# A two-layer network on one core: the carried states of a scan multiplied in 16-bit halves instead of float32

## The chip, the core and the metric

The kernel runs on one core of a Trainium2 chip. The metric is the time of the whole program on the device in microseconds (us), as the median of several runs. Five engines work side by side and meet at semaphores: TensorE (PE; its weight loads are shown apart, as PEld), VectorE (DVE), ScalarE (ACT), GpSimd (POOL) and SyncE (SP), which issues the DMAs.

## The reference

Four blocks follow each other, each one `x = layernorm(x + block(x))`: a Mamba2 mixer, a linear layer with dequantised weights, an attention with rotary positions, and a gated feed-forward. The change lies in the mixer. It has 2 sequences of 512 tokens, 128 heads of 64 channels in 8 groups, and chunks of 128 tokens:

```
dt  = clip(softplus(dt + dt_bias));  cs = cumsum(dt * A) in each chunk
xdt = x * dt
Ydiag  = (C B^T * exp(cs_l - cs_s), lower triangle) @ xdt
states = B^T @ (exp(cs_last - cs) * xdt)             # one per chunk and head
carry  = carry * exp(cs_last) + states               # from chunk to chunk
Yoff   = (C * exp(cs)) @ carry of the chunks before
Y = Ydiag + Yoff + x * D
```

After it come a gate `Y * silu(z)`, an RMS norm over a group and the output projection. The change is in how `Yoff` is multiplied: `C * exp(cs)` is the decayed C, `carry` the carried state.

## The kernel before

The mixer walks over 128 tiles. A tile is 128 channels (two heads) of one sequence, 512 tokens in 4 chunks. Eight tiles make a unit (one group, one sequence), two units a group of 16 tiles. Each engine has its own program of *slots*, one per tile (`slots`, line 672): slot 0, then a hardware loop of 7 rounds over `m = 1..16`, then 15 more. I call `m % 16` the slot's number. Each engine's order inside a slot is written out by hand, and semaphores alone tie the engines together.

TensorE in slot m: `scan(m)` (line 802) makes Y of tile m in PSUM. For each chunk it has one float32 product for each head with the matrix E (`Ydiag`, line 811, 128x64 weights and 128 columns), and, from the second chunk on, one for each head with the carried state `st` as weights and the decayed C `ecs` as columns (`Yoff`, line 815). The two heads take the left and right 64 columns of the array. Then `states(m+1)` (nine 16-bit products from `xw` and its rest `xwlo`), the x projection of tile m+3 (12 products of 512 columns), the z projection (`gate(m+1)`, 12), `turn_x(m+2)` (4 transposes), in slots 2 and 10 the B projection, in 4 and 12 the C projection (12 more each), and the output projection of tile m-1 (12). A float32 operand is taken as two 16-bit halves in these projections: `lead(w)` is the upper half of each word as bfloat16, `rest(w)` an fp16 remainder, and `product` (line 57) makes three 16-bit products of them.

VectorE in slot m (line 1171): waits for `y_ready` of `scan(m)`, `u = x*D + Y` (1176), `state(m+1, 0)` (1115), `u = u*gz` (1181), `state(m+1, 1..2)` (1120), E times the masked CB (`masked`, 1109), then `taps`: three convolution steps (256) with `remainder` (the rest of y, 1199) behind the first and `turned_x(m+2)` (x times dt, 1128) behind the second. In slots 0 and 8 it also adds the previous unit's output to the residual (1148), in 2, 4, 10 and 12 it has three more convolution steps, for B or C.

ScalarE in slot m (line 1023): in even slots two exponentials of E (996) behind a table load; the square of u (1002), `leading` (1005: y's leading half), in slots 0 to 7 the leading half of an output weight (230), the first convolution tap (243), eight `decays` (990), the gate's SiLU (1009, which gives `gz`, behind a table load in even slots), and the SiLU of x (248), which waits for the third convolution step.

GpSimd in slot m (line 1311): `decayed_C(m+1)` (1280, in place in `ecs`), in slots 0 to 7 the rest of an output weight (226), the sum of squares (1297), weight splits of the next group (`split`, 209: wx in slots 7 to 14, wz in 9 to 16), then `decayed_x(m+2)` (1285 `xw`, 1289 `xwlo`), which waits for `turned_x(m+2)` and which TensorE's `states(m+2)` needs in slot m+1. In the last unit (slots 120 to 127) `tail` adds the making of the linear layer's weights (lines 579 to 600).

`st` has two buffers, `ecs` four, E four, `xt` and `xw` two. `scan(m)` waits for E (`m_done`), the decayed C (`cs_done`) and `gz`.

Of the kernel before, what the change touches and what calls it, by code (L numbers as in the profile page):

```python
# [33 lines left out]
def lead(words):  # L34

    return words.bitcast(BF16)[..., 1::2]
# [594 lines left out]
def mixer(k, io, sc, aw):  # L631
# [3 lines left out]
    with ExitStack() as tmp:  # L635
        def sb(name, shape, dt=F32):
            return k.sb(name, shape, dt, tmp)
# [1 line left out]
        E = [sb(f"E{i}", [P, 2, CH, P]) for i in range(4)]  # L639
        xt = [sb(f"xt{i}", [P, CH, P]) for i in range(2)]  # L640
        xw = [sb(f"xw{i}", [P, CH - 1, P]) for i in range(2)]
        st = [sb(f"st{i}", [P, CH - 1, P]) for i in range(2)]
        u = [sb(f"u{i}", [P, T]) for i in range(2)]
        gz = [sb(f"gz{i}", [P, T]) for i in range(2)]
        yhi = [sb(f"yhi{i}", [P, T], F16) for i in range(2)]
# [3 lines left out]
        cbm = [sb(f"cbm{i}", [P, CH, P]) for i in range(NB)]  # L649
        bthi, btlo = ([sb(f"bt{n}{i}", [P, CH - 1, P], F16) for i in range(NB)] for n in ("hi", "lo"))  # L650
        xwlo = [sb(f"xwlo{i}", [P, CH - 1, P], F16) for i in range(2)]
        ms, rstd = sb("ms", [P, CH]), sb("rstd", [P, CH])
        lin = Linear(k, io, sc, (cbm[0][:].rearrange("p c t -> p (c t)"), acc[0][:]), tmp)
        norms = lin.norms
# [10 lines left out]
        ms_done, evac_done = S("ms_done"), S("evac_done")  # L665

        cs_done, xw_done, acc_done, rstd_done = S("cs_done"), S("xw_done"), S("acc_done"), S("rstd_done")
        acc_split, xw_lo, bt_done = S("acc_split"), S("xw_lo"), S("bt_done")

        Y, W, OUT = k.bank[2], k.bank[3], k.bank[4:8]  # L670
# [35 lines left out]
        with nc.Block() as block:  # L706
# [94 lines left out]
            def _(pe):  # L801
                def scan(t):

                    pe.wait_ge(m_done, t.n + 1)
                    pe.wait_ge(cs_done, t.n + 1)
                    pe.wait_ge(gz_done, t.n + 1)
                    for c in range(CH):
                        cols = slice(c * P, (c + 1) * P)
                        for h in range(2):
                            r = slice(h * HD, (h + 1) * HD)  # L810
                            mm = nc.tensor.matmul(Y[r, cols], xt[t.i % 2][:, c, r], E[t.i % 4][:, h, c], start=True, stop=c == 0,  # L811
                                                  skip_group_check=True)
                        for h in range(2 if c else 0):
                            r = slice(h * HD, (h + 1) * HD)
                            mm = nc.tensor.matmul(Y[r, cols], st[t.i % 2][:, c - 1, r], sc.ecs[t.i % 4][:, h, (c - 1) * P:c * P],  # L815
                                                  start=False, stop=True, skip_group_check=True)
                    mm.then_inc(y_ready, 1)

                def states(t):
# [164 lines left out]
            def _(act):  # L984
# [9 lines left out]
                def exps(t):  # L994
                    act.wait_ge(clip_done, t.n + 1)
                    nc.scalar.activation(E[t.i % 4][:], E[t.i % 4][:], ACT.Exp, scale=-1.0).then_inc(exp_done, 1)

                def square(t):
                    act.wait_ge(yg_done, t.n + 1)
                    if t.i:  # L1000
                        act.wait_ge(acc_done, t.n)
                    nc.scalar.activation((sq if t.i else acc[t.b])[:], u[t.i % 2][:], ACT.Square).then_inc(sq_done, 1)  # L1002
# [12 lines left out]
                def first():  # L1015
                    decays(tile_at(0, 0))
                    turned_B(tile_at(0, 0), OUT[3])
                    exps(tile_at(0, 0))
                    gate(tile_at(0, 0))
                    decays(tile_at(0, 1))  # L1020
                    decays(tile_at(0, 2))

                def slot(g, m):
                    s = tile_at(g, m)
                    if m % 2 == 0:
                        for d in (1, 2):
                            if tile_at(g, m + d):
                                exps(tile_at(g, m + d))
                    square(s)
                    leading(s)  # L1030
                    if m % 16 < XT:

                        sc.lead_wo(act, s.g, m % 16)
                    t, nu = tile_at(g, m + 3), next_unit(s)
                    if t:
                        q = conv_of_slot(s, "x")

                        wait(act, y_done, s.n)
                        sc.tap(act, q, ring_bank(s.b, x_use(s)), sc.xc[t.i % 4], t.g, t.b, 2 + t.i)
                        if not (isinstance(g, int) and g == 0 and m == 0):  # L1040
                            decays(t)
                    if tile_at(g, m + 1):
                        gate(tile_at(g, m + 1))
                    if t:
                        sc.silu(act, q, sc.xc[t.i % 4])
                    if isinstance(g, int) and g == 0 and m == 0:
                        decays(t)
                    if nu and s.i == 2:
                        act.wait_ge(bt_ready, s.u + 1)
                        sc.tap(act, conv_of_slot(s, "B"), ring_bank(s.b, USE_B), sc.xcB, nu.g, nu.b, 0)  # L1050
                        sc.silu(act, conv_of_slot(s, "B"), sc.xcB)
                    if nu and s.i == 4:
                        sc.tap(act, conv_of_slot(s, "C"), ring_bank(s.b, USE_C), sc.xcC[nu.b], nu.g, nu.b, 1)
                        sc.silu(act, conv_of_slot(s, "C"), sc.xcC[nu.b])
                    if nu and s.i == 6:
                        turned_B(nu, k.bank[ring_bank(s.b, USE_BT)])
                    if is_last_unit(s):
                        tail(s)
# [45 lines left out]
            def _(dve):  # L1104
# [7 lines left out]
                def state(t, c):  # L1112
                    if c == 0:
                        dve.wait_ge(st_ready, t.n + 1)
                        nc.vector.tensor_copy(st[t.i % 2][:, 0], W[:, 0:P]).then_inc(s_step, 1)
                        return
                    dve.wait_ge(s_step, 3 * t.n + c)
                    for h in range(2):
                        r = slice(h * HD, (h + 1) * HD)
                        mm = nc.vector.scalar_tensor_tensor(  # L1120
                            out=st[t.i % 2][:, c, r], in0=st[t.i % 2][:, c - 1, r], scalar=head(sc.cd, t, c, h),
                            in1=W[:, c * P + h * HD:c * P + (h + 1) * HD], op0=ALU.mult, op1=ALU.add)
                    mm.then_inc(s_step, 1)

                def turned_x(t):

# [33 lines left out]
                def first():  # L1160
                    dve.sem_inc(ms_done, 1)
                    dve.sem_inc(evac_done, 4)
                    turned_x(tile_at(0, 0))
                    masked_CB(tile_at(0, 0), ring_bank(1, USE_CB))
                    rest_of_B(tile_at(0, 0), OUT[3])
                    for c in range(CH - 1):
                        state(tile_at(0, 0), c)
                    masked(tile_at(0, 0))
                    turned_x(tile_at(0, 1))

                def slot(g, m):
# [10 lines left out]
                    if n1:  # L1182
                        state(n1, 1)
                        state(n1, 2)
                        masked(n1)
                    if ended:
                        mean_square(s.u, s.b)

# [11 lines left out]
                                                       in1=yhi[s.i % 2][:], op0=ALU.mult, op1=ALU.subtract).then_inc(lo_done, 1)  # L1200

                    if n3:
                        taps("x", sc.xc[n3.i % 4], n3, 2 + n3.i, (remainder, lambda: turned_x(n2)))
                    else:
                        remainder()
                        if n2:
                            turned_x(n2)
# [67 lines left out]
            def _(pool):  # L1275
                def decayed_C(t):
                    pool.wait_ge(sc.ecs_in[t.i % 2], (t.g * 8 + (t.b * 4 + t.i // 2 + 1)) * 16)
                    pool.wait_ge(sc.xc_done, conv_of_C(t) + 1)
                    e = sc.ecs[t.i % 4]
                    nc.gpsimd.tensor_tensor(e[:], e[:], sc.xcC[t.b][:, P:T].unsqueeze(1).to_broadcast([P, 2, T - P]),  # L1280
                                            ALU.mult).then_inc(cs_done, 1)

                def decayed_x(t):
                    pool.wait_ge(xt_done, t.n + 1)
# [26 lines left out]
                def slot(g, m):  # L1311
# [9 lines left out]
                    if more:  # L1321
                        if mm == 4:
                            sc.split_bc(pool, s.g + 1, 0)
                        if mm == 6:
                            sc.split_bc(pool, s.g + 1, 1)
                        if 7 <= mm <= 14:
                            sc.split_wx(pool, s.g + 1, mm - 7)
                        if 9 <= mm:
                            sc.split_wz(pool, s.g + 1, mm - 9)
                    if m == 16:  # L1330
                        sc.split_wz(pool, s.g, XT - 1)
                    if tile_at(g, m + 2):
                        decayed_x(tile_at(g, m + 2))
                    if is_last_unit(s):
                        tail(s)

# [1031 lines left out]
```

## Time and profile before

| | us |
|---|---|
| median of 3 runs (lowest, highest) | 2432.82 (2430.52, 2433.77) |
| the profiled execution | 2433.26 |
| its span, first to last instruction | 2431.4 |
| busy in the span: PE, DVE, ACT, POOL | 2343.2 (96%), 1794.1 (74%), 1584.3 (65%), 1377.3 (57%) |

The trace's timeline gives the start of each scan. These are the starts in one round of the loop, for slot numbers 0 to 15 and the next 0, in us from the span's start: 970.69, 981.66, 992.46, 1005.72, 1016.22, 1029.32, 1040.71, 1051.54, 1062.04, 1072.74, 1083.25, 1096.34, 1106.84, 1119.94, 1131.33, 1142.16, 1152.67. So a plain slot lasts 10.50 us, one with a B or C projection 13.09 to 13.26, slots 5 and 13 last 11.39, 6 and 14 10.83, 8 10.70, and 0 and 1 10.97 and 10.80. The mixer runs from about 57 us to 1515 us, the linear layer to 1560, attention and feed-forward to the end.

How to read it: busy times of one engine overlap a little (an instruction starts before the one before it has ended), and a PE that is busy is only one whose pipeline holds something. What a slot costs is the distance between two scan starts.

### The profile page before, as it was taken

The numbers are of one execution on the slowest core, as the hardware profiler recorded it, in microseconds if no ns is written. First come the engines' busy times: TensorE is split into PE (matmuls) and PEld (weight loads), VectorE is DVE, ScalarE is ACT, GpSimd is POOL, SyncE is SP. The second block draws the span as 40 slices with busy tenths as digits, with TensorE's granted clock in tenths as the row PEclk, the third lists the DMA queues.
The fourth block names the chain that finished last, engine by engine and source line by source line (L and its number), as shares of the span: only waits on it lengthen the run. The fifth ranks groups of instructions, "written<-read, shape, count | busy, mean of one in ns | idle before, by whom it ended". The sixth has DMA issues, their size and how long they took to land. (4 is left out here: it accounts for less than half of the span.)

```text
span 2431.4 us, 49850 instructions
## 1 busy us (share of the span) xinstructions
PE 2343.2 (96%) x16008; PEld 1328.4 (55%) x16008; DVE 1794.1 (74%) x3250; ACT 1584.3 (65%) x3327; POOL 1377.3 (57%) x1178
## 2 busy tenths in 40 slices
PE   6999999999999999999999998879999999999898
PEld 3555555555555555555555554445555556555444
DVE  6777777777777787777777885567787777888613
ACT  6776776776776776776776774355665555655533
POOL 5576576576576576576576579344344434454323
PEclk8999999999999999999999999889999999999999
DMA  7343343343343343343343441320010110100000
GB/s 244 120 134 113 111 136 113 112 137 111 111 137 111 110 136 113 112 137 111 112 137 110 132 152 36 129 89 14 36 40 14 41 36 14 40 10 14 1 1 35
DMA packets 117294, 218.95 MB, mean 90 GB/s; under 512 B 10016, under 2 KB 43424, under 8 KB 115840
## 3 DMA queue, kind: packets, MB, share of 16 engines
q1 hardware_dynamic: 116992, 215.29, 27.0%
q8 instruction: 145, 2.38, 0.4%
q14 instruction: 157, 1.29, 0.2%
HBM read 212.10 MB, written 3.15 MB: 89 GB/s over the span
## 5 line engine op out<-in xcount | busy, mean ns | idle before, releaser
L990 ACT ACTIVATE E<-wq,cst 128x128 f32<-128x128 f32 x1024 | 311.7, 389 | 2.2 <-PEq L298 2.2
L256 DVE SCALAR_TENSOR_TENSOR xc<-bank,taps,xc 128x511 f32<-128x511 f32 (+2 forms) x384 | 283.0, 737 | 24.6 <-ACT xc L243 24.1
L1963 POOL TENSOR_TENSOR qT<-qT,qrot 128x512 f32<-128x512 f32 x64 | 81.3, 1270 | 358.3 <-DVE qrot L1852 358.3
L1297 POOL TENSOR_TENSOR acc<-acc,sq 128x512 f32<-128x512 f32 x112 | 162.6, 1452 | 183.5 <-ACT sq L1002 183.5
L61 PE MATMUL bank<-xhi,wx 128*128 128x512 f16 x640 | 242.7, 379 | 0.0
L60 PE MATMUL bank<-xlo,wx 128*128 128x512 f16 x640 | 242.6, 379 | 0.0
L59 PE MATMUL bank<-xhi,wx 128*128 128x512 f16 x640 | 242.5, 379 | 0.0
L1109 DVE TENSOR_TENSOR E<-E,cbm 128x1024 f32<-128x1024 f32 x128 | 235.0, 1836 | 0.9
L1280 POOL TENSOR_TENSOR ecs<-ecs,xcC 128x768 f32<-128x768 f32 x128 | 235.2, 1837 | 0.4 <-POOLq L298 0.4
L1176 DVE SCALAR_TENSOR_TENSOR u<-xc,D,bank 128x512 f32<-128x512 f32 x128 | 95.7, 747 | 177.1 <-PE bank L815 166.4
L1285 POOL TENSOR_TENSOR xw<-xt,wdec 128x384 f32<-128x384 f32 x128 | 106.5, 832 | 174.5 <-DVE xt L1128 174.4
L811 PE MATMUL bank<-E,xt 128*64 128x128 f32 x2048 | 185.6, 280 | 14.6 <-issue 7.3
L1002 ACT ACTIVATE sq<-u 128x512 f32<-128x512 f32 x112 | 70.5, 629 | 196.8 <-DVE u L1181 195.5
L59 PE MATMUL bank<-xhi,wz 128*128 128x512 f16 x512 | 195.3, 381 | 0.4 <-DVE u L1176 0.3
L60 PE MATMUL bank<-xlo,wz 128*128 128x512 f16 x512 | 195.2, 381 | 0.0
L61 PE MATMUL bank<-xhi,wz 128*128 128x512 f16 x512 | 195.1, 381 | 0.0
L59 PE MATMUL bank<-wohi,yhi 128*128 128x512 bf16 x512 | 194.2, 379 | 0.0
L60 PE MATMUL bank<-wolo,yhi 128*128 128x512 f16 x512 | 194.2, 379 | 0.0
L61 PE MATMUL bank<-wohi,ylo 128*128 128x512 bf16 x512 | 194.2, 379 | 0.0
L1780 ACT ACTIVATE probs<-bank,nmx 128x512 f32<-128x512 f32 (+3 forms) x256 | 131.5, 526 | 67.6 <-DVE nmx L1882 67.6
L811 PEld LDWEIGHTS bank<-E,xt 128*64 128x64 f32 x2048 | 120.2, 137 | 64.6 <-issue 62.1
L209 POOL TENSOR_TENSOR wx<-wx 128x512 f16<-128x512 f32 x80 | 147.7, 1850 | 10.5 <-DMA wx<-in_w_xbc 10.5
(265 smaller groups left out, 6617.3 us busy)
## 6 DMA issues: line engine op xcount, KB each, us to landing
wq<-cs_rows SPq DMA_DIRECT2D x128, 512.0 KB, 4.0
ecs<-ecs_rows SPq DMA_DIRECT2D x128, 384.0 KB, 3.6
wx<-in_w_xbc SPq DMA_DIRECT2D x80, 256.0 KB, 2.6
wz<-in_w_z SPq DMA_DIRECT2D x64, 256.0 KB, 2.6
wo<-in_w_o SPq DMA_DIRECT2D x64, 256.0 KB, 3.9
wq<-in_wq SPq DMA_DIRECT2D x8, 1024.0 KB, 5.6
awo_raw<-in_wo SPq DMA_DIRECT2D x32, 256.0 KB, 3.0
wkv<-in_wkv SPq DMA_DIRECT2D x8, 512.0 KB, 3.7
```

Of the source, the lines that this page charges most:

```text
L59: nc.tensor.matmul(out, lhs[0], rhs[0], start=first, stop=False, skip_group_check=skip)
L60: nc.tensor.matmul(out, lhs[0], rhs[1], start=False, stop=False, skip_group_check=skip)
L61: return nc.tensor.matmul(out, lhs[1], rhs[0], start=False, stop=last, skip_group_check=skip)
L209: self.nc.gpsimd.tensor_tensor(rest(w), w, lead(w), ALU.subtract).then_inc(sem, 1)
L256: self.nc.vector.scalar_tensor_tensor(out=dst[:, d:T], in0=self.k.bank[bank][:, 0:T - d], scalar=self.taps[:, bass.ds(g, 1), b, j, 3 - d:4 ...
L811: mm = nc.tensor.matmul(Y[r, cols], xt[t.i % 2][:, c, r], E[t.i % 4][:, h, c], start=True, stop=c == 0, skip_group_check=True)
L990: ins = nc.scalar.activation(E[t.i % 4][:, h, c], sc.csr[t.i % 2][:, h, c * P:(c + 1) * P], ACT.Relu, scale=-1.0, bias=head(sc.cst, t, c, h))
L1109: nc.vector.tensor_tensor(e, e, cbm[t.b][:].rearrange("p c t -> p (c t)").unsqueeze(1).to_broadcast([P, 2, T]), ALU.mult).then_inc(m_done, 1)
L1280: nc.gpsimd.tensor_tensor(e[:], e[:], sc.xcC[t.b][:, P:T].unsqueeze(1).to_broadcast([P, 2, T - P]), ALU.mult).then_inc(cs_done, 1)
L1285: nc.gpsimd.tensor_tensor(by_head(xw[t.i % 2][:]), by_head(xt[t.i % 2][:, 0:CH - 1]), of_heads(sc.wdec, t, 0, CH - 1), ALU.mult).then_inc( ...
L1297: nc.gpsimd.tensor_tensor(acc[t.b][:], acc[t.b][:], sq[:], ALU.add).then_inc(acc_done, 1)
L1780: ins = nc.scalar.activation(pr[h % 2][:, P_OFF[i]:P_OFF[i] + (i + 1) * P], k.bank[bank][:, at:at + (i + 1) * P], ACT.Exp, bias=nmx[h % 2] ...
```

## The change

The carried states and the decayed C are each split into two 16-bit halves, and the two float32 products for a chunk become six 16-bit ones, in the order head 0, head 1 for each of three terms. The halves of the state are made on ScalarE (`sthi`, fp16) and VectorE (`stlo`, fp16), the rest of the decayed C on GpSimd (`ecslo`, fp16; its leading half is read in place). `st`, `sthi`, `stlo` and `ecslo` have one buffer each. On VectorE `turned_x` moves from behind the second convolution step to behind the first, and `remainder` from the first to the second. On GpSimd `decayed_x` moves ahead of the split of wz.

```diff
-        st = [sb(f"st{i}", [P, CH - 1, P]) for i in range(2)]
+        st = sb("st", [P, CH - 1, P])
+        sthi, stlo = sb("sthi", [P, CH - 1, P], F16), sb("stlo", [P, CH - 1, P], F16)
...
+        ecslo = sb("ecslo", [P, 2, T - P], F16)
...
                 def scan(t):
                     pe.wait_ge(m_done, t.n + 1)
-                    pe.wait_ge(cs_done, t.n + 1)
+                    pe.wait_ge(cs_lo, t.n + 1)
+                    pe.wait_ge(st_lo, t.n + 1)
                     pe.wait_ge(gz_done, t.n + 1)
...
-                        for h in range(2 if c else 0):
-                            r = slice(h * HD, (h + 1) * HD)
-                            mm = nc.tensor.matmul(Y[r, cols], st[t.i % 2][:, c - 1, r], sc.ecs[t.i % 4][:, h, (c - 1) * P:c * P],
-                                                  start=False, stop=True, skip_group_check=True)
+                        e, d = sc.ecs[t.i % 4], slice((c - 1) * P, c * P)
+                        for x in range(3 if c else 0):
+                            for h in range(2):
+                                r = slice(h * HD, (h + 1) * HD)
+                                mm = nc.tensor.matmul(Y[r, cols], (sthi, sthi, stlo)[x][:, c - 1, r],
+                                                      (lead(e[:, h, d]), ecslo[:, h, d], lead(e[:, h, d]))[x],
+                                                      start=False, stop=x == 2, skip_group_check=True)
...
+                def leading_states(t):
+                    act.wait_ge(s_step, 3 * t.n + 3)
+                    nc.scalar.copy(sthi[:], st[:]).then_inc(st_hi, 1)
...
                     square(s)
                     leading(s)
+                    if tile_at(g, m + 1):
+                        leading_states(tile_at(g, m + 1))
...
+                def rest_of_states(t):
+                    dve.wait_ge(st_hi, t.n + 1)
+                    nc.vector.tensor_tensor(stlo[:], st[:], sthi[:], ALU.subtract).then_inc(st_lo, 1)
...
                         masked(n1)
+                        rest_of_states(n1)
...
-                        taps("x", sc.xc[n3.i % 4], n3, 2 + n3.i, (remainder, lambda: turned_x(n2)))
+                        taps("x", sc.xc[n3.i % 4], n3, 2 + n3.i, (lambda: turned_x(n2), remainder))
...
                     nc.gpsimd.tensor_tensor(e[:], e[:], sc.xcC[t.b][:, P:T].unsqueeze(1).to_broadcast([P, 2, T - P]),
                                             ALU.mult).then_inc(cs_done, 1)
+                    pool.wait_ge(cs_done, t.n + 1)
+                    wait(pool, y_ready, t.n)
+                    nc.gpsimd.tensor_tensor(ecslo[:], e[:], lead(e[:]), ALU.subtract).then_inc(cs_lo, 1)
...
-                        if 9 <= mm:
-                            sc.split_wz(pool, s.g + 1, mm - 9)
+                    if tile_at(g, m + 2):
+                        decayed_x(tile_at(g, m + 2))
+                    if more and 9 <= mm:
+                        sc.split_wz(pool, s.g + 1, mm - 9)
                     if m == 16:
                         sc.split_wz(pool, s.g, XT - 1)
-                    if tile_at(g, m + 2):
-                        decayed_x(tile_at(g, m + 2))
```

## Rows read from the trace of the kernel before

**Rows 1.** Stretches, us: length, busy PE, PEld, DVE, ACT, POOL; clock, DMA share, GB/s

```profile
970.69:1152.67 181.98, 181.46 (x1320) 102.77 (x1319) 140.51 (x234) 133.52 (x259) 119.55 (x93) 1.00 0.39 120
1436.32:1493.85 57.53, 50.59 (x379) 28.98 (x378) 43.15 (x73) 35.14 (x68) 54.95 (x50) 1.00 0.33 112
```

**Rows 2.** Timeline of PE in slot 3: start, duration, line, operation, [idle before it]

```profile
1005.72 0.66 PE L811 MATMUL bank<-E,xt 128*64 128x128 f32 x8
1006.21 0.39 PE L815 MATMUL bank<-ecs,st 128*64 128x128 f32 x4
1006.42 0.39 PE L811 MATMUL bank<-E,xt 128*64 128x128 f32 x4
...
1007.47 0.22 PE L60 MATMUL bank<-xwlo,bthi 128*128 128x128 f16 x1
1007.52 0.22 PE L61 MATMUL bank<-xw,btlo 128*128 128x128 bf16 x1
```

**Rows 3.** Weight loads and a matmul by line: ns least, median, most; first and last start

```profile
L815 PEld LDWEIGHTS bank<-ecs,st x1536: 136/137/231, 57.7 to 1510.5; 128*64 128x64 f32 x192
L815 PE MATMUL bank<-ecs,st x1536: 272/273/421, 57.8 to 1510.6; 128*64 128x128 f32 x192
L861 PEld LDWEIGHTS bank<-xcC,xcB x128: 189/192/337, 47.6 to 1404.0; 128*128 128x128 f32 x128
```

**Rows 4.** Timeline of ACT in slot 8 (scan starts at 1062.04)

```profile
1061.71 0.63 ACT L248 ACTIVATE xc<-xc 128x512 f32<-128x512 f32 x1 [1.21 <-DVE xc L256]
1063.65 2.01 ACT L996 ACTIVATE E<-E 128x1024 f32<-128x1024 f32 x2
1065.56 0.61 ACT L1002 ACTIVATE acc<-u 128x512 f32<-128x512 f32 x1
1066.09 0.70 ACT L1005 ACTIVATE yhi<-u,nw 128x512 f16<-128x512 f32 x1
1067.39 0.78 ACT L243 ACTIVATE xc<-bank,taps 128x512 f32<-128x512 f32 x1 [0.60 <-PE bank L61]
1068.07 2.43 ACT L990 ACTIVATE E<-wq,cst 128x128 f32<-128x128 f32 x8
1071.82 0.60 ACT L1009 ACTIVATE gz<-bank 128x512 f32<-128x512 f32 x1
```

**Rows 5.** Timeline of DVE in slots 8 and 9 (scans start at 1062.04, 1072.74)

```profile
1063.93 0.75 DVE L1176 SCALAR_TENSOR_TENSOR u<-xc,D,bank 128x512 f32<-128x512 f32 x1 [2.25 <-PE bank L815]
1064.79 0.68 DVE L1181 TENSOR_TENSOR u<-u,gz 128x512 f32<-128x512 f32 x1
...
1074.66 0.75 DVE L1176 SCALAR_TENSOR_TENSOR u<-xc,D,bank 128x512 f32<-128x512 f32 x1 [0.30 <-PE bank L815]
```

**Rows 6.** Timeline of POOL and DVE where two of their instructions meet, slot 2

```profile
994.21 1.83 POOL L1280 TENSOR_TENSOR ecs<-ecs,xcC 128x768 f32<-128x768 f32 x1
...
995.24 1.35 DVE L1181 TENSOR_TENSOR u<-u,gz 128x512 f32<-128x512 f32 x1
```

**Rows 7.** The nearest instructions to the added ones, by line

```profile
L1289 POOL TENSOR_TENSOR xwlo<-xw x128: 825/826/829, 49.7 to 1495.8; 128x384 f16<-128x384 f32 x128
L226 POOL TENSOR_TENSOR wolo<-wo x64: 1038/1040/1958, 61.4 to 1417.1; 128x512 f16<-128x512 f32 x64
L1138 DVE TENSOR_TENSOR btlo<-bank,bthi x16: 557/558/560, 50.9 to 1415.3; 128x384 f16<-128x384 f32 x16
L1013 ACT CAST bthi<-bank x16: 469/471/478, 50.4 to 1414.8; 128x384 f16<-128x384 f32 x16
```

**Rows 8.** Timeline of PE: the scan of slot 2, behind slot 1

```profile
992.46 0.66 PE L811 MATMUL bank<-E,xt 128*64 128x128 f32 x8 [0.23 <-ACT gz L1009]
```

**Rows 9.** Timeline of POOL and PE before the last scans

```profile
1491.94 1.80 POOL L1280 TENSOR_TENSOR ecs<-ecs,xcC 128x768 f32<-128x768 f32 x1
...
1507.23 1.80 POOL L1280 TENSOR_TENSOR ecs<-ecs,xcC 128x768 f32<-128x768 f32 x1
...
1493.85 1.12 PE L811 MATMUL bank<-E,xt 128*64 128x128 f32 x8 [5.67 <-issue]
```

More of the change, by code:

```diff
@@ L667, in mixer @@
         cs_done, xw_done, acc_done, rstd_done = S("cs_done"), S("xw_done"), S("acc_done"), S("rstd_done")
+        st_hi, st_lo, cs_lo = S("st_hi"), S("st_lo"), S("cs_lo")
         acc_split, xw_lo, bt_done = S("acc_split"), S("xw_lo"), S("bt_done")
@@ L1019, in first @@
                     gate(tile_at(0, 0))
+                    leading_states(tile_at(0, 0))
                     decays(tile_at(0, 1))
@@ L1114, in state @@
                         dve.wait_ge(st_ready, t.n + 1)
-                        nc.vector.tensor_copy(st[t.i % 2][:, 0], W[:, 0:P]).then_inc(s_step, 1)
+                        nc.vector.tensor_copy(st[:, 0], W[:, 0:P]).then_inc(s_step, 1)
                         return
@@ L1120, in state @@
                         mm = nc.vector.scalar_tensor_tensor(
-                            out=st[t.i % 2][:, c, r], in0=st[t.i % 2][:, c - 1, r], scalar=head(sc.cd, t, c, h),
+                            out=st[:, c, r], in0=st[:, c - 1, r], scalar=head(sc.cd, t, c, h),
                             in1=W[:, c * P + h * HD:c * P + (h + 1) * HD], op0=ALU.mult, op1=ALU.add)
                     mm.then_inc(s_step, 1)
+                def rest_of_states(t):
+                    dve.wait_ge(st_hi, t.n + 1)
+                    nc.vector.tensor_tensor(stlo[:], st[:], sthi[:], ALU.subtract).then_inc(st_lo, 1)
                 def turned_x(t):
@@ L1168, in first @@
                     masked(tile_at(0, 0))
+                    rest_of_states(tile_at(0, 0))
                     turned_x(tile_at(0, 1))
```

## The prediction

> **What bounds the kernel now.** I read the stretches first [rows 1]: in one round of the mixer's loop (16 slots, 181.98 us) PE is busy 181.46 us, DVE 140.5, ACT 133.5, POOL 119.6. So PE sets the time, and an instruction added elsewhere costs nothing while something covers it. In the last unit it is different: in slots 121 to 125 (57.53 us) POOL is busy 54.95 and PE 50.59. Then I read single slots in the timelines, because the shares of a round hide a chain that is nearly as long as a slot: scan, DVE's u, ACT's square and y, first tap, eight decays, gz, next scan. In slot 8 gz ends at 1071.82 + 0.60 = 1072.42 and the scan starts at 1072.74, 0.32 later; the chain's other slack is the 0.60 that ACT waits for PE's projection before the first tap [rows 4]. Behind slot 1 the scan already waits for gz [rows 8]. DVE has 2.25 us of rest before u in slot 8, but only 0.30 in slot 9, behind the residual adds [rows 5].
>
> **The change, part by part.**
>
> *PE.* The 4 records of one chunk's float32 products (two heads, two records each) take from 1006.21 to 1006.42, 0.21 to 0.22 us [rows 2]. Four of them span 0.39 us: 0.11 from the first pair to the second, 0.273 for one record [rows 3], nearly nothing left for a distance inside a pair. So the two heads' halves of the array run side by side. In 16 bits a product of 128 columns takes 1007.52 - 1007.47, 0.05 to 0.06 us [rows 2]. If the pairs stay side by side, three terms take 3 x 0.057 = 0.17 against 0.218: 0.047 saved on each of 3 chunks, 0.14 us a slot. Bounds: below, 6 x 0.057 = 0.34 a chunk if the two heads run one behind the other, 0.37 us lost a slot; above, 3 x 0.05, 0.2 us gained. I take 0.14, the row of 16-bit products with the pairing of the float32 ones.
>
> What speaks against it are the weight loads. A float32 load of 128 columns is 192 ns, one of 64 columns 137 [rows 3]: 55 ns for 64 columns, just under one product's 57. The Trainium skill (TensorEngine Tiling, Restrictions and Gotchas) says that tiling the columns switches the fast weight load off. By that rule the new loads take the 55 ns too, hidden only if both heads load at once; no row here shows a 64-column load in 16 bits. Loaded one behind the other they would give 6 x 55 = 0.33 us a chunk, which is rival C.
>
> *ACT.* `leading_states` is a copy of 128x384 into fp16. The nearest row is 471 ns, out of PSUM [rows 7]; its neighbours overlap by about 0.05 to 0.1, so 0.42 net (0.38 to 0.5). It stands ahead of the first tap, in the chain above.
>
> *DVE.* `rest_of_states` is 128x384, near the 558 ns of btlo [rows 7], 0.50 net (0.4 to 0.6), and more where POOL holds it up. It stands behind `masked` and ahead of all taps.
>
> *POOL.* ecslo is 768 elements. From 384 to 512 elements this form grows from 826 to 1040 ns [rows 7], 1.67 ns an element, so 768 take 0.826 + 384 x 0.00167 = 1.47 us (1.3 to 1.83, the latter being the multiply of 768 elements [rows 6]). By its new wait it starts when scan(m) is done or, in the slots where `decayed_C` comes late, when that has ended. Behind the wait are queued the output weight's split, the sum of squares, the wx split and `decayed_x`. They have POOL's rest to fall into: 181.98 - 119.55 = 62 us a round, against 16 x 1.53 = 24.
>
> *The two meet.* In slot 2 `u*gz` takes 1.35 instead of 0.68 us while POOL's tensor_tensor runs from 994.21 to 996.04; it ends at 996.59, 0.55 behind POOL [rows 5, 6]. So VectorE's operation with two operands in SBUF waits until POOL's has ended and then needs its 0.55. ecslo starts at the end of the scan, and `u*gz` 0.86 us after u starts. Put into slot 8: scan ends at about 1063.8, ecslo holds until 1065.3 or, behind a late `decayed_C`, 1066.2; `u*gz` ends at 1065.85 to 1066.75 instead of 1065.47. That is 0.4 to 1.3 us, 0.8 in the middle, in almost every slot. I find nothing that excludes it.
>
> *The two moves.* `turned_x` a place earlier gives xw 0.7 to 0.8 us sooner, and the wz split no longer stands in front of it. That pays back what DVE's lateness takes from `states`. `remainder` is needed a slot later and costs nothing. But the third convolution step still ends behind all of it, and with it the SiLU of x, after which ACT begins the next slot. The added waits of the scan for `cs_lo` and `st_lo` cost nothing outside the last unit: ecslo ends some 3 to 5 us, stlo some 8 to 9 us into a slot of 10.4.
>
> **The sum.** Slot 8, worked out: in slot 7 DVE's third step ends later by 0.8 (behind ecslo) and 0.5 (stlo), its 2.25 us of rest hides that for u, but not for the SiLU; less 0.14 for the shorter scan this is 1.2. ACT's SiLU, table load and exponentials, which end at 1065.66 [rows 4], end at 1066.9; square, y and the new copy bring the first tap to 1066.9 + 0.53 + 0.62 + 0.42 = 1068.5 + 0.1, against 1067.39: 1.2 late. Of that 0.32 is covered before the scan, so slot 8 grows by 0.9. The others by the same steps: slot 6, where the longer slot 5 covers the SiLU but the copy of the output weight fills the 0.60, 0.7; slot 14, without that copy, 0.3; slot 0, as 8 but with it, 1.2; slot 1, where nothing is covered and DVE comes late from the residual, 1.4; slot 10, where DVE, late since slot 9's 0.30 of rest [rows 5], gives xw late for `states`, 0.8; slot 12, 0.3. Together 5.6. In the other 9 slots PE keeps its 0.14: -1.3. So 4.3 us a round, and for the 120 slots before the last unit 7.5 x 4.3 = 32.
>
> In the last unit scan 126 starts at 1493.85, 0.11 after `decayed_C` [rows 9], behind 5.67 us of idle PE. Here ecslo is straight in the path: 6 of them from slot 121 on, 6 x 1.53 = 9.2, less some 1.7 of the 2.58 us that POOL has free there [rows 1]: 7.5 us. (Bounds 6 and 10.)
>
> The profiled execution took 2433.26 us, 1.9 more than its span and 0.4 more than the median, which I leave aside. 2433.3 + 32 + 7.5 = 2473 us.
>
> **The rivals.**
>
> *B: the cover holds.* ecslo and `u*gz` don't keep each other waiting as in rows 6, or the chain has more slack than I found. Then PE's gain is all that is left: 120 x 0.14 = 17 us less, 7.5 more at the end: 2424 us. If the last unit hides its share too, 2415. For it: PE's share of a round and the free time of all the others [rows 1]. Against it: slot 8's 0.32 and the wait behind slot 1 [rows 4, 8].
>
> *C: the 16-bit pairs are slower than float32.* Loads or columns of the two heads behind each other: 0.33 a chunk is 0.11 more than before, 0.34 a slot, and 0.48 more than I took. In the 9 slots in which PE sets the time this is 4.3 us a round, 32 in all, of which about a third is given back where the other chains wait for the same PE: 2495 us. Against it: the float32 pairs run side by side [rows 2, 3].
>
> *D: a wash.* ecslo comes early enough in half of the slots and the copies overlap more than I think: 4.3 falls to about -1 a round, 2433.3 - 8 + 7.5 = 2433 us.
>
> The point from which the sign turns: the slots lose 5.6 us a round against PE's 16 x 0.14 = 2.3. With a loss of 1.3 a round the last unit's 7.5 just balances the gain.
>
> **How the numbers follow.** The forecast has 0.62, its own range 2452 to 2502: below, copies at 0.38 and 0.4 and ecslo at 1.3, which take some 2.5 us off a round; above, ecslo at 1.83, which puts POOL itself behind in slots 9 to 14, where wx and wz are both split, some +3.5 a round. B has 0.17, C 0.10, D 0.08, and 0.03 is left to something slower still. A change of 0.2%, 4.9 us, is about what can be told from none. Faster 0.18 (B), same 0.07 (most of D), slower 0.75. The range reaches down to B, as only so 8 in 10 is held, and up to the forecast's bound: 2422 to 2502.
>
> **What would show it.** The records of the three terms, 18 a tile, 64 columns wide: right if pairs start 0.05 to 0.06 us apart, C if 0.11. `u*gz` near 1.1 to 1.9 us instead of 0.68, and ending 0.55 after ecslo: the contention is right. Scan starts in a round: slot 8 at 11.6 instead of 10.70, 3, 7, 9, 15 at 10.36, the round near 186.3 instead of 181.98. Behind slots 0, 1, 6 and 8 the scan's wait ends with gz. In the last unit the scans 126 and 127 start 0.1 us after an ecslo, and the stretch from scan 120 on is some 7.5 us longer. The prediction is wrong if `u*gz` keeps to 0.68, or if the rounds are shorter than 181.98.

## The result and the profile after

The changed kernel takes 2476.25 us (median of four runs) against 2432.27 for the kernel before on the same chip; the recorded ratio is 1.0174, 95% interval 1.0159 to 1.0188. One of the four runs took 8239.14 us, was disturbed and is left out of the ratio (the other three are 2475.83, 2475.89 and 2476.61), as is one of 12170.60 us of the kernel with the copy alone below. The profiled execution has a span of 2474.0 us, 42.6 longer than before. The engines' totals, from the page of the changed kernel (busy us, share of the span, instructions):

```profile
PE 2320.4 (94%) x16579; PEld 1324.8 (54%) x16776; DVE 1974.7 (80%) x3378; ACT 1627.7 (66%) x3455; POOL 1613.8 (65%) x1306
```

I cut the span at three scans. From scan 0 to scan 120 it grew from 1368.3 to 1405.0 us (+36.7), from scan 120 to scan 127 from 83.5 to 94.0 (+10.5), and the rest shrank from 922.3 to 917.6 (-4.6). That rest lies behind the mixer; over all kernels built here it varies between 916.5 and 922.3 without a pattern that I can name, so I leave it aside. The windows answering to [rows 1] are slots 80 to 95 and, here, scan 120 to scan 127 (columns as there):

```profile
996.41:1183.93 187.52, 178.95 (x1400) 101.82 (x1415) 164.11 (x251) 138.69 (x274) 148.97 (x109) 1.00 0.37 116
1462.38:1556.35 93.97, 74.01 (x567) 43.32 (x574) 70.54 (x108) 56.06 (x102) 86.09 (x75) 0.93 0.26 87
```

The reader is to see that PE works less (178.95 against 181.46 us) in a longer round: it idles 8.6 us where it idled 0.5. DVE has 23.6 us more work and POOL 29.4. Between 240 and 1370 us PE stands idle for 45.6 us in all, where it was 4.0: 33.1 of them wait for gz, 4.7 for DVE's btlo, 4.2 for POOL's xwlo and 3.6 for DVE's u. In the last stretch POOL is busy 86.1 of 94.0.

Now the single steps. PE in slot 83, the timeline that answers to [rows 2]:

```profile
1033.24 0.66 PE L815 MATMUL bank<-E,xt 128*64 128x128 f32 x8
1033.72 0.23 PE L821 MATMUL bank<-ecs,sthi 128*64 128x128 bf16 x2
1033.78 0.22 PE L821 MATMUL bank<-ecslo,sthi 128*64 128x128 f16 x2
1033.84 0.23 PE L821 MATMUL bank<-ecs,stlo 128*64 128x128 bf16 x2
1033.90 0.39 PE L815 MATMUL bank<-E,xt 128*64 128x128 f32 x4
```

The pairs start 0.06 apart, and a chunk takes 0.18 us (1033.90 - 1033.72) against 0.21. The two heads do run side by side.

DVE in slot 87, the scan of which starts at 1079.79:

```profile
1081.55 0.75 DVE L1195 SCALAR_TENSOR_TENSOR u<-xc,D,bank 128x512 f32<-128x512 f32 x1 [0.42 <-PE bank L821]
1082.21 0.28 DVE L1129 COPY st<-bank 128x128 f32<-128x128 f32 x1
1082.41 1.70 DVE L1200 TENSOR_TENSOR u<-u,gz 128x512 f32<-128x512 f32 x1
1084.03 1.07 DVE L1134 SCALAR_TENSOR_TENSOR st<-st,cd,bank 128x64 f32<-128x64 f32 x4
1085.03 2.30 DVE L1123 TENSOR_TENSOR E<-E,cbm 128x1024 f32<-128x1024 f32 x1
1087.24 1.39 DVE L1141 TENSOR_TENSOR stlo<-st,sthi 128x384 f16<-128x384 f32 x1
...
1091.38 0.73 DVE L256 SCALAR_TENSOR_TENSOR xc<-bank,taps,xc 128x509 f32<-128x509 f32 x1
1092.03 0.73 DVE L1195 SCALAR_TENSOR_TENSOR u<-xc,D,bank 128x512 f32<-128x512 f32 x1
```

and POOL beside it:

```profile
1082.09 1.47 POOL L1304 TENSOR_TENSOR ecslo<-ecs 128x768 f16<-128x768 f32 x1
1083.52 1.49 POOL L226 TENSOR_TENSOR wolo<-wo 128x512 f16<-128x512 f32 x1
1084.97 1.27 POOL L1320 TENSOR_TENSOR acc<-acc,sq 128x512 f32<-128x512 f32 x1
1086.32 1.91 POOL L1323 TENSOR_TENSOR acc<-acc 128x512 bf16<-128x512 f32 x1
```

ecslo ends at 1083.56 and `u*gz` at 1084.11, 0.55 later, as in [rows 6]. But the same happens to stlo: it lies beside the sum of squares' split (ends 1088.23) and itself ends at 1088.63. This is no accident of one slot: of the 128 stlo 90 take over 0.64 us, and all 90 end 0.41 us after an instruction of POOL; of the 128 `u*gz` 85 take over 0.78, and all of them end 0.54 to 0.55 after one. The third convolution step starts at 1091.38, and DVE goes from it straight into the next slot's u: the 2.25 us of rest of [rows 5] are gone. What follows on ACT in slot 88, against [rows 4]:

```profile
1092.14 0.63 ACT L248 ACTIVATE xc<-xc 128x512 f32<-128x512 f32 x1 [2.34 <-DVE xc L256]
...
1097.13 0.49 ACT L1007 CAST sthi<-st 128x384 f16<-128x384 f32 x1
1097.54 0.77 ACT L243 ACTIVATE xc<-bank,taps 128x512 f32<-128x512 f32 x1
1098.21 2.43 ACT L997 ACTIVATE E<-wq,cst 128x128 f32<-128x128 f32 x8
1100.66 1.28 ACT L1020 ACT_TABLE_LOAD   x1
1101.95 0.60 ACT L1020 ACTIVATE gz<-bank 128x512 f32<-128x512 f32 x1
```

The scan of slot 88 starts at 1090.15, the SiLU of x 1.99 later; in [rows 4] it started 0.33 before its scan. gz ends at 1102.55 and the next scan follows at 1102.70. Over all slots the durations (ns, least, median, most), answering to [rows 7], are:

```profile
L1141 DVE TENSOR_TENSOR stlo<-st,sthi x128: 543/1390/1925, 56.6 to 1549.4; 128x384 f16<-128x384 f32 x128
L1304 POOL TENSOR_TENSOR ecslo<-ecs x128: 1467/1469/2328, 49.2 to 1554.8; 128x768 f16<-128x768 f32 x128
```

And the waits of PE for gz between 240 and 1370 us (us in total, times, longest), before and after:

```profile
PE bank L811 <- ACT gz L1009: 3.5, 9, 0.7
```

```profile
PE bank L815 <- ACT gz L1020: 33.1, 34, 1.4
```

### The profile page after: what moved, and what is told of

It is laid out like the page before. It is cut to its first block and busy times, and to the rows that moved or that the text cites. A ratio compares the mean times of both kernels' runs of the same rounds, so it can differ in the third digit from the quotient of the medians.

```text
span 2474.0 us, 51933 instructions
## 1 busy us (share of the span) xinstructions
PE 2320.4 (94%) x16579; PEld 1324.8 (54%) x16776; DVE 1974.7 (80%) x3378; ACT 1627.7 (66%) x3455; POOL 1613.8 (65%) x1306
## 5 line engine op out<-in xcount | busy, mean ns | idle before, releaser
L1320 POOL TENSOR_TENSOR acc<-acc,sq 128x512 f32<-128x512 f32 x112 | 191.1, 1706 | 61.6 <-ACT sq L1013 61.6
L1304 POOL TENSOR_TENSOR ecslo<-ecs 128x768 f16<-128x768 f32 x128 | 209.2, 1634 | 32.8 <-PE bank L821 24.3
L1123 DVE TENSOR_TENSOR E<-E,cbm 128x1024 f32<-128x1024 f32 x128 | 222.5, 1739 | 0.4 <-ACT E L1003 0.4
L248 ACT ACTIVATE xc<-xc 128x512 f32<-128x512 f32 x128 | 80.2, 628 | 147.1 <-DVE xc L256 146.9
L815 PEld LDWEIGHTS bank<-E,xt 128*64 128x64 f32 x2048 | 111.4, 138 | 110.7 <-issue 107.6
L1141 DVE TENSOR_TENSOR stlo<-st,sthi 128x384 f16<-128x384 f32 x128 | 153.7, 1201 | 19.2 <-ACT sthi L1007 19.2
```

The lines of the kernel that those rows point to most:

```text
L1123: nc.vector.tensor_tensor(e, e, cbm[t.b][:].rearrange("p c t -> p (c t)").unsqueeze(1).to_broadcast([P, 2, T]), ALU.mult).then_inc(m_done, 1)
L1141: nc.vector.tensor_tensor(stlo[:], st[:], sthi[:], ALU.subtract).then_inc(st_lo, 1)
L1304: nc.gpsimd.tensor_tensor(ecslo[:], e[:], lead(e[:]), ALU.subtract).then_inc(cs_lo, 1)
L1320: nc.gpsimd.tensor_tensor(acc[t.b][:], acc[t.b][:], sq[:], ALU.add).then_inc(acc_done, 1)
```

## The experiments

All ratios are to the kernel before on the same chip, with 95% intervals. "Slots" below is the time from scan 0 to scan 120 in the profiled execution, "last unit" from scan 120 to scan 127; before has 1368.3 and 83.5. Both come from one execution of each kernel, and the executions of one kernel lie up to 8 us apart, so differences of 1 to 3 us in them can't be told from none. The diffs are shortened; a line without code says in words what goes or comes.

Of the twelve expectations only that for TensorE's part with the old orders came out within its range. The others missed by 1 to 42 us, nine of the eleven by being too low.

**TensorE's part alone.** From the changed kernel all three added instructions are taken out and st has two buffers again; both moves stay. This kernel, the next three and the one with the old orders leave out the rests' part of the result, all or some of it; they are built for their time alone.

```diff
+ sh = lead(st[t.i % 2][:])
- (sthi, sthi, stlo)[x][:, c - 1, r], (lead(e[:, h, d]), ecslo[:, h, d], lead(e[:, h, d]))[x]
+ sh[:, c - 1, r], lead(e[:, h, d])        # in all three terms
- leading_states, rest_of_states, ecslo and their waits
```

> The change with TensorE's part alone: all three 16-bit terms are issued, but each multiplies the leading halves of state and decayed C, read in place; no sthi, stlo or ecslo is made (their terms' values are left out), the two moves stay. Theory (PE gains 0.14 us a slot, the loss of the change comes from what is made on the other three engines): 128 x 0.14 = 18 us under before, 2415 us, plain slots 10.36. Rival (the shorter scan is worth nothing, or the moves themselves cost): 2433 or more. Against the changed kernel this isolates 61 us of cost of the three makers.

Measured: 2427.85 us, 0.9974 [0.9965, 0.9984]. Slots 1366.4, last unit 83.1. Faster, by less than PE's arithmetic should give; what eats it is found below.

The next three kernels put one instruction back each.

```diff
+ pool.wait_ge(cs_done, t.n + 1); wait(pool, y_ready, t.n)
+ nc.gpsimd.tensor_tensor(ecslo[:], e[:], lead(e[:]), ALU.subtract).then_inc(cs_lo, 1)
```

> As pe_only, with GpSimd's ecslo as in the change (with its wait for the scan) and used in its term; state halves still only the leading ones. Theory (ecslo holds u*gz up in most slots, and is straight in the path of the last unit): some 8 to 10 us at the end, and of the 0.8 us in the chain most is covered by the 0.9 us of slack while nothing else is added: 2424 to 2430 us. Rival (GpSimd's instruction is the whole loss): 2470.

Measured: 2436.52 us, 1.0011 [1.0001, 1.0020]. Slots 1368.1, only 1.7 over the kernel without it; last unit 92.6, 9.5 over it. By the medians of the runs the whole program is 8.7 us over it, so the last unit holds all of the cost. `u*gz` is held up as forecast:

```profile
L1187 DVE TENSOR_TENSOR u<-u,gz x128: 673/1168/1947, 61.9 to 1523.0; 128x512 f32<-128x512 f32 x128
```

Its median is 1168 ns, longer than in the full change (1008), and yet the slots grow by no more than can be told from none. The hold-up is real and nearly free by itself: DVE still waits 55.4 us for PE ahead of u between 240 and 1370 us, so its rest can take it up.

```diff
+ dve.wait_ge(s_step, 3 * t.n + 3)
+ nc.vector.tensor_tensor(stlo[:], st[t.i % 2][:], lead(st[t.i % 2][:]), ALU.subtract).then_inc(st_lo, 1)
```

> As pe_only, with VectorE's stlo (from the state less its leading half, read in place) made and used; no copy on ScalarE, no ecslo. Theory: 0.55 us a slot on VectorE, longer behind GpSimd's splits, mostly in VectorE's rest: 2417 to 2425 us; the SiLU of x is later but the chain's slack holds. Rival (VectorE is the bound and stlo the whole loss): 2455 or more.

Measured: 2450.37 us, 1.0069 [1.0052, 1.0086]. Slots 1380.9, 14.5 over the kernel without it; last unit 86.5, 3.4 over it; by the medians the whole program is 22.5 over it. This one instruction is the dearest, and it is as long as in the full change although no ecslo runs here:

```profile
L1133 DVE TENSOR_TENSOR stlo<-st x128: 544/1391/1639, 57.2 to 1520.0; 128x384 f16<-128x384 f32 x128
```

The work that holds it up is POOL's other work, not ecslo: in the full change the long ones lie beside the sum of squares (42 of 90) or the split of wx (23), and one beside ecslo.

```diff
+ act.wait_ge(s_step, 3 * t.n + 3)
+ nc.scalar.copy(sthi[:], st[t.i % 2][:]).then_inc(st_hi, 1)     # read by nothing
```

> As pe_only, with ScalarE's copy of the state to fp16 made in the change's place but not used. Theory: 0.42 us in the chain, covered except behind slots 0 and 1 and where the output weight's copy stands beside it: 2 to 4 us over pe_only, 2417 to 2419. Rival (ScalarE's chain is the bound in every even slot): 64 x 0.42 = 27 over, 2442.

Measured: 2436.65 us, 1.0014 [1.0004, 1.0024]. Slots 1377.0: 10.6 for the copy ahead of the first tap (8.8 for the whole program, by the medians).

**The moves.** First the full change with both moves undone:

```diff
- taps("x", ..., (lambda: turned_x(n2), remainder))
+ taps("x", ..., (remainder, lambda: turned_x(n2)))
- decayed_x(...) ahead of split_wz
+ decayed_x(...) behind split_wz
```

> The changed kernel with the order of before on VectorE (remainder behind the first step, turned_x behind the second) and on GpSimd (wz split ahead of decayed_x). Theory of the prediction: the moves pay back late xw, so without them it is slower, by some 10 to 15 us (2487 to 2491), mostly in slots with a wx and a wz split. What the first four runs suggest against it: in pe_only VectorE waits 76 us in all for TensorE's transposes before turned_x, so the move costs where VectorE is early; then 2470 or less.

Measured: 2478.57 us, 1.0181 [1.0164, 1.0198]. Beside 2476.25 the moves are worth nothing that can be told, but the waits are others. Between 240 and 1370 us PE waits, with the moves undone,

```profile
PE bank L59 <- POOL xwlo L1312: 22.3, 24, 1.7
PE bank L815 <- ACT gz L1020: 14.3, 17, 1.1
```

and in the change:

```profile
PE bank L59 <- POOL xwlo L1312: 4.2, 7, 0.6
```

with the 33.1 for gz shown above. So the moves do bring xw sooner: they take 18.1 us of waiting away there and put 18.8 in front of gz instead. The move on VectorE and that on GpSimd were not tried one without the other. Then the kernel before with the two moves and nothing else (the reverse of this diff):

> The kernel before with the two moves alone. Prediction's theory: nothing, 2433 +- 2. Theory formed from pe_only (only 6 us faster instead of 18, slots 7 and 15 at 10.79 instead of 10.36): turned_x now stands in front of two convolution steps and waits for the transposes, the third step and the SiLU behind it come 0.7 us later, and slots 0, 1, 7, 8, 15 grow: 1 to 1.5 us a round, 2441 to 2445.

Measured: 2440.21 us, 1.0026 [1.0015, 1.0037]; slots 1376.0, 7.7 more than before. So the moves alone cost time. The wait is new; between 240 and 1370 us of this kernel:

```profile
ACT xc L248 <- DVE xc L256: 123.7, 87, 2.3
DVE xt L1128 <- PE bank L833: 69.1, 80, 1.3
```

`turned_x`, a place earlier, now stands in front of TensorE's transposes (L833) and DVE waits 0.86 us in 80 slots. The third step is queued behind it, and ACT's SiLU waits for that 123.7 us, where it waited 53.3 before.

**Where ecslo lies.** The residual is written over ecs in place, so the wait for the scan before is not needed:

```diff
- wait(pool, y_ready, t.n)
- nc.gpsimd.tensor_tensor(ecslo[:], e[:], lead(e[:]), ALU.subtract)
+ nc.gpsimd.tensor_tensor(rest(e[:]), e[:], lead(e[:]), ALU.subtract)
```

> The changed kernel with the decayed C's rest written into the lower halves of its own words, so that it needs no wait for the scan and follows decayed_C at once. Theory (the loss is that ecslo runs just when u*gz wants the port): in the slots where decayed_C runs before the scan's end ecslo is now over before u*gz, in the others nothing changes; one to two us a round less, 2462 to 2468. Rival (the wait is the cost, by what queues behind it): 2455 or less. Rival (GpSimd's order is no matter): 2476.

Measured: 2474.11 us, 1.0168 [1.0151, 1.0185]; slots 1403.0, 2.0 less than the change. The added wait on POOL costs nothing that can be told. (The kernel that shifts ecslo altogether follows below.)

**No copy on ACT.** The leading half of st is read in place, stlo is st less that half:

```diff
- nc.scalar.copy(sthi[:], st[:])
- nc.vector.tensor_tensor(stlo[:], st[:], sthi[:], ALU.subtract)
+ nc.vector.tensor_tensor(stlo[:], st[t.i % 2][:], lead(st[t.i % 2][:]), ALU.subtract)
```

> The changed kernel without ScalarE's copy: the leading half of the state is read in place as bfloat16, stlo is the state less that, two buffers of st. All values made. Theory: pe_copy costs 9 us over pe_only and stlo's wait for the copy goes: 10 to 15 us under the changed kernel, 2461 to 2466. If the costs of copy, stlo and ecslo simply add up (9 + 22 + 9 over pe_only = 2468): 2459.

Measured: 2467.75 us, 1.0142 [1.0125, 1.0159]; slots 1391.5, 13.5 less than the change, last unit 94.2. Against TensorE's part with the moves both residuals together cost 25.1, where alone they cost 1.7 and 14.5: ecslo is 10.6 beside stlo. The 13.5 are not the copy's time alone: with it go st's single buffer and stlo's wait for the copy, 14.7 us between 240 and 1370 us of the change.

**TensorE's part with the old orders.** As the first kernel, but with both moves undone.

> pe_only with the order of before on VectorE and GpSimd: nothing but TensorE's 16-bit terms on the leading halves (the rests' values are left out). Theory: the plain slot gains its 0.14 everywhere, slots 7 and 15 go back from 10.79 to 10.36: 18 us under before, 2415 to 2419 us, and moves_only's 6 us over before is found here too as the distance to pe_only (2427.9). Rival (the shorter scan is worth only half, because the chain through ScalarE is the bound in slots 0, 1 and 8 anyway): 2424.

Measured: 2416.40 us, 0.9930 [0.9913, 0.9946]. This is PE's gain by itself: slots 1354.7, 13.6 less than before. A plain slot takes 10.37 where it took 10.50. With the moves (the first kernel) 11.7 of these 13.6 are lost again.

**ecslo at the end of POOL's slot**, in place and behind the sum of squares, so that it no longer follows `decayed_C`:

```diff
+ def rest_of_C(t): ... nc.gpsimd.tensor_tensor(rest(e[:]), e[:], lead(e[:]), ALU.subtract)
+ # in the slot, behind accumulate and root:
+ rest_of_C(tile_at(g, m + 1))
```

> The changed kernel with the decayed C's rest made in place and behind GpSimd's sum of squares, when u*gz is long done. Theory (the cost of ecslo is that it holds u*gz, which heads the chain square, y, tap, gz): u*gz is back at 0.68 us, slots 0, 6, 8, 14 shrink by 0.5 to 0.8, round 187.4 to 184 or 185: 2450 to 2460 us. Rival (not the place but the sum of GpSimd's and VectorE's shared time counts; E and stlo are held up instead): 2470 to 2476.

Measured: 2498.76 us, 1.0264 [1.0247, 1.0281], 22.5 slower than the change. The kernel doesn't test what it was built for: `u*gz` was not freed, its mean between 80 and 1400 us is 1310 ns, against 1190 in the change. It shows only that this later place is worse than the one ahead of `u*gz`. Between 250 and 1400 us TensorE now waits for xwlo, 22.4 us of PE's time where it was 4.2 in the change (PEld's 30.4 overlap with them):

```profile
PEld bank L59 <- POOL xwlo L1313: 30.4, 43, 1.3
PE bank L59 <- POOL xwlo L1313: 22.4, 30, 1.1
```

**A first try at a better version.** No copy; both residuals in place and on POOL, late; DVE's old order, POOL's `decayed_x` ahead of the wz split; float32 products in the last unit.

```diff
+ nc.gpsimd.tensor_tensor(rest(w), w, lead(w), ALU.subtract).then_inc(st_lo, 1)   # w = st[t.i % 2][:]
+ if whole(t): float32 st x ecs        # last unit
```

> All values made: the state's leading half read in place (no copy), its rest made by GpSimd in place behind the late ecslo, VectorE's order as before, GpSimd's decayed_x ahead of the wz split, and the last unit's carried part in float32 as before (no halves there). Theory: VectorE is back to its old work, ScalarE too, GpSimd has 2.3 us a slot more of its 62 us of rest a round, the last unit costs nothing: near pe_no_moves, with some 0.3 us a slot of contention: 2420 to 2430 us, at or under before. Rival (GpSimd's load makes xw late and holds E and the y remainder): 2440 or more.

Measured: 2472.18 us, 1.0155 [1.0138, 1.0172]. Last unit 83.5, so the float32 products there take the 10.5 us away. The slots stay at 1408.0. The trace shows PE waiting between 240 and 1370 us for xwlo here too, 16.6 us, and 14.0 for the state's rest, which POOL now makes; gz costs 7.0. That POOL stands idle behind the late `turned_x`, with two residuals queued in front, is argued, not tested.

**Another order on VectorE, and no copy.** stlo on DVE but between first and second tap, `turned_x` between second and third, and the remainder of y behind the third; POOL's old order; float32 products in the last unit. All work of the slots but the copy is there. stlo still stands ahead of the third convolution step; what went behind it is the remainder.

```diff
- rest_of_states(n1)                    # behind masked(n1)
- taps("x", ..., (lambda: turned_x(n2), remainder))
+ taps("x", ..., (lambda: rest_of_states(n1), lambda: turned_x(n2)))
+ remainder()
```

> All values made. From the changed kernel: the state's leading half read in place (no copy on ScalarE); on VectorE stlo stands behind the first convolution step, turned_x behind the second as before, and the remainder of y behind the third, so that the path to the third step holds stlo instead of the remainder; GpSimd's order as before (wz split ahead of decayed_x); the last unit's carried part in float32. Theory formed from the runs (what costs is whatever delays the third step and with it ScalarE's SiLU, table load and chain; the last unit's 10 us are GpSimd's ecslo): near pe_no_moves' 2416 plus ecslo's 2 and 2 to 6 of contention on the shared port: 2420 to 2426 us, 0.3 to 0.6% under before. Rival (the port that VectorE's two-operand work and GpSimd share is the bound, in whatever order; best ran at 2472 with the same sum of work): 2445 or more.

Measured: 2431.06 us (median of 11 runs), 0.9990 [0.9981, 0.9999]; slots 1367.6, last unit 83.3. This is 45 us under the change and level with the kernel before, short of the hoped-for gain. Beside the kernel without the copy (1391.5 and 94.2) the new orders are worth 23.9 us in the slots, the float32 products 10.9 in the last unit. Its slot 87 on DVE:

```profile
1053.24 0.87 DVE L1208 TENSOR_TENSOR u<-u,gz 128x512 f32<-128x512 f32 x1
1054.04 1.08 DVE L1140 SCALAR_TENSOR_TENSOR st<-st,cd,bank 128x64 f32<-128x64 f32 x4
1055.03 1.49 DVE L1129 TENSOR_TENSOR E<-E,cbm 128x1024 f32<-128x1024 f32 x1
1056.72 0.75 DVE L256 SCALAR_TENSOR_TENSOR xc<-bank,taps,xc 128x511 f32<-128x511 f32 x1 [0.20 <-ACT xc L243]
1057.39 0.55 DVE L1149 TENSOR_TENSOR stlo<-st 128x384 f16<-128x384 f32 x1
...
1059.22 0.74 DVE L256 SCALAR_TENSOR_TENSOR xc<-bank,taps,xc 128x509 f32<-128x509 f32 x1
1059.88 0.86 DVE L1226 SCALAR_TENSOR_TENSOR ylo<-u,nw,yhi 128x512 f16<-128x512 f32 x1
1062.73 0.75 DVE L1203 SCALAR_TENSOR_TENSOR u<-xc,D,bank 128x512 f32<-128x512 f32 x1 [1.99 <-PE bank L834]
```

stlo takes 0.55 here (728 ns in the median, 1390 in the change), the remainder no longer stands ahead of the third step, and DVE has 1.99 us of rest again. `u*gz`, though, is as slow as in the change, 1181 ns in the mean between 80 and 1400 us against 1190: so its hold-up by itself is not what the change loses by. The wait for gz, and that of the SiLU for the third step (112.7 us in the change), are back where they were:

```profile
ACT xc L248 <- DVE xc L256: 53.7, 60, 1.6
PE bank L822 <- ACT gz L1029: 3.1, 9, 0.5
```

## Why the prediction came out right, and where its steps did not

The forecast was 2473 us with +32 in the slots and +7.5 in the last unit; measured 2476, with +36.7 and +10.5, and -4.6 behind the mixer, which I had not forecast and can't explain. So the mixer grew by 47.2 for the 39.5 forecast, and the -4.6 hides over half of that error, by luck. The mechanism stands in the main: PE's small gain is lost because DVE's and ACT's added work lies ahead of the third step and the first tap, and the scan then waits for gz (33.1 of PE's 45.6 us of idle time). Against TensorE's part with the moves the slots' cost is this (us over 120 slots):

| kernel | 0 to 120 | over TensorE's part with the moves | PE's wait for gz |
|---|---|---|---|
| TensorE's part, old orders | 1354.7 | -11.7 | 2.4 |
| TensorE's part, with the moves | 1366.4 | 0 | 5.5 |
| + ecslo | 1368.1 | +1.7 | 6.8 |
| + copy | 1377.0 | +10.6 | 17.2 |
| + stlo | 1380.9 | +14.5 | 16.6 |
| + ecslo and stlo | 1391.5 | +25.1 | 19.9 |
| the change | 1405.0 | +38.6 | 33.1 |
| the same work, reordered, no copy | 1367.6 | +1.2 | 3.1 |

The last row has POOL's old order and `turned_x` in its old place, so its fair measure is the first row: the added work still costs 12.9 there. The moves undone in the full change (1406.2) are 51.5 over that row.

Step by step:

- *PE, 0.14 us a slot.* Right: pairs 0.06 apart, a plain slot 10.37 instead of 10.50, 13.6 us over 120 slots instead of 17. Rival C is refuted. Its loads do appear. A 16-bit load of 64 columns takes 107 to 110 ns, one of 128 columns 96, one of 64 columns in float32 137 [rows 3]:

```profile
L821 PEld LDWEIGHTS bank<-ecslo,sthi x768: 108/110/178, 57.9 to 1558.4; 128*64 128x64 f16 x192
L59 PEld LDWEIGHTS bank<-xw,bthi x384: 95/96/151, 53.3 to 1542.7; 128*128 128x128 f16 x192
```

  Half the columns take longer, which agrees with the Trainium skill (TensorEngine Tiling (Array Packing), Restrictions and Gotchas), by which column tiling switches the fast weight load off; but as the pairs still start 0.06 us apart, the longer loads cost nothing here.
- *ACT's copy, 0.42 net.* Right in size (0.49 as recorded, 0.41 to the next start). It costs 10.6 us over the 120 slots alone, and 13.5 go with it when it is taken out of the change.
- *ecslo, 1.47 us.* Right where it runs free: least 1467, median 1469 ns. Its mean is 1634, as DVE holds it up too: 63 of the 128 take over 1.5 us, and all of them end 1.32 to 1.33 after a `u*gz`. Between 80 and 1400 us the median is 1792. The bounds (1.3 to 1.83) hold both. Its wait for the scan before: 2.0 us, nothing that can be told, as said.
- *`u*gz` held up by 0.4 to 1.3 us.* Right as a fact (median 0.68 before, 1.01 after, mean 0.81 and 1.19), wrong as the main cost. Alone it costs 1.7 us in 120 slots, and the reordered kernel, level with the one before, has it in full.
- *stlo, 0.50 net.* The worst-sized term. Beside POOL's sum of squares and splits it takes 1.39, about 0.9 more than forecast, in the median slot, and costs 14.5 us alone. I had written "more where POOL holds it up" and then summed 0.5. The error in this term and that in `u*gz` have opposite signs, and the sum came out near by that, which is luck. The parts measured one by one don't add up either: PE's gain, the moves, ecslo, copy and stlo give -13.6 + 11.7 + 1.7 + 10.6 + 14.5 = 24.9, and the change has 36.7. The 11.8 between them come of the parts' meeting, for which the sum has no term.
- *The moves "pay back" and cost nothing.* The first half is right: undone, they leave PE 22.3 us of waiting for xwlo instead of 4.2. The second half failed: +7.7 us on the kernel before, +11.7 on top of PE's gain, where `turned_x` in front of the transposes makes DVE wait 63.5 us. In the full change that wait is 1.1 us, but gz then costs 18.8 more than without the moves, as much as they save at xwlo.
- *Slots.* Growth in slots 80 to 95, forecast and measured: slot 1 1.4 and 1.43, slot 6 0.7 and 0.91, slot 12 0.3 and 0.56, slot 0 1.2 and 0.67, slot 8 0.9 and 1.84 here but 1.2 to 1.3 in other rounds, slot 14 0.3 and 1.13, slot 10 0.8 and -0.14. The cost of slot 10 was to come from a late xw; it is there with the moves undone (1.68 us of waiting for xwlo in that slot), so the moves took it away. Slot 7, forecast to shrink, shrank here but grew by 0.5 to 0.8 in four of the eight times that it comes. In the other nine -0.14 was forecast; 3, 15 and 2 had +0.11, +0.19 and -0.31, the others -0.13 or -0.14. The round grew by 5.5 here, by 4.9 as the mean of the 7.5 rounds before the last unit, for the 4.3 forecast.
- *The last unit, 7.5 (6 to 10).* 10.5 measured, just outside the bounds. The mechanism is as drawn: scan 126 starts 0.10 after ecslo's end.

```profile
1537.75 1.47 POOL L1304 TENSOR_TENSOR ecslo<-ecs 128x768 f16<-128x768 f32 x1
```

```profile
1539.32 0.69 PE L815 MATMUL bank<-E,xt 128*64 128x128 f32 x4 [7.02 <-issue]
```

  ecslo alone gives 9.5 of it. The error has two halves. There are seven ecslo in the stretch and not six, and they take 11.7 us together, where I had 9.2. And of POOL's free time they took up 1.0 (8.9 before, 7.9 after) for the 1.7 that I took off. POOL's other work did not get longer there, 76.5 us summed over its instructions against 76.3.

What stays open: why reordering still leaves 15 us against TensorE's part with the old orders; which of the differences of the reordered kernel (stlo's place, the remainder behind the third step, `turned_x` and POOL's order as before) does how much; how the 11.8 us arise that the parts don't have alone; and the -4.6 behind the mixer.

## What to carry to other kernels

Before adding an instruction to an engine with rest, find the one instruction of the slot that another engine waits for (here the third convolution step), and count what is put ahead of it. Taking the remainder from there, and stlo to a place where POOL held it up less, gave back 24 us of slots; no run shows which of the two, or the old places of `turned_x` and `decayed_x`, did it. The added work was still not free, 13 us. Price an elementwise operation with two operands in SBUF by what the other engine on those operands runs beside it, not by its shortest record. Then test moves by themselves: two moves that were neutral inside the change cost 8 to 12 us alone, and TensorE's gain of 0.7% came in full only with the old orders (0.3% with the moves).

## What the hardware showed that I had not expected

DVE's subtraction out of SBUF (stlo) has a least of 544 and a median of 1391 ns with no new work on POOL at all, while the taps, which read PSUM, stay at 0.73 to 0.75 in both kernels. The Trainium skill (GPSIMD Engine Reference, Specifications) names contention between GpSimd and VectorE's instructions with two SBUF inputs; the traces agree, and show that it goes by whole instructions: all 90 long stlo of the change end 0.41 us after an instruction of POOL, all 85 long `u*gz` 0.54 to 0.55. It goes the other way too: in the change the split of the output weight on POOL takes 1.49 in slot 87, where 1.04 was the median before [rows 7], and the long ecslo end 1.32 us after DVE's `u*gz`, which had started first. And the costs of such operations didn't add in this kernel: ecslo 1.7 us alone and 10.6 beside stlo.
